# Where the transform's way back stands: beside attention's small scores, with attention's transposes in an experts' bank

## The reference, cut to what matters

```
x = x + xattn(LN(x), ctx)     # top-32 cross attention -> film -> FFT convolution -> film -> FFN
x = x + attn(LN(x))           # self attention over 32 tokens, one head, width 256
x = x + ffn(LN(x))            # 8 experts, top-2 gates, all experts computed
```

## Time and profile before

| | us |
|---|---|
| median of 3 runs | 606.03 |
| lowest and highest | 601.78, 606.12 |
| profiled execution | 601.4 |
| its span, first to last instruction | 599.6 |
| PE busy in the span | 551.3 |
| DVE busy | 498.0 |
| ACT busy | 293.2 |
| POOL busy | 280.6 |
| mean granted TensorE clock | 0.979 |

### The profile page before, as it was taken

How to read it: one execution, slowest core, us unless ns; L and a number is a source line. 1 busy time by engine, 2 the same in 40 slices (tenths; PEclk the granted TensorE clock), 3 DMA queues, 4 the chain that set the end, 5 groups by cost and what they waited for, 6 DMA issues and landing times.

```text
span 599.6 us, 13084 instructions
## 1 busy us (share of the span) xinstructions
PE 551.3 (92%) x4558; PEld 399.3 (67%) x4558; DVE 498.0 (83%) x1761; ACT 293.2 (49%) x768; POOL 280.6 (47%) x656
## 2 busy tenths in 40 slices
PE   3688488999999999999999999999999999989966
PEld 2344264768686777768686768686877768675845
DVE  7997876789898988989888989898988989876443
ACT  3032242464646564555646364646564555635432
POOL 6755147625445362626363535445362636262521
PEclk9998897999999999999999999999999999999998
DMA  8488103030403030210303030304030210000000
GB/s 282 65 325 338 66 2 119 2 113 2 131 2 131 1 110 22 74 60 23 109 19 113 19 113 10 123 1 131 3 129 3 83 50 10 2 10 1 10 1 17
DMA packets 17957, 42.33 MB, mean 71 GB/s; under 512 B 2770, under 2 KB 9570, under 8 KB 17380
## 3 DMA queue, kind: packets, MB, share of 16 engines
q1 hardware_dynamic: 17892, 41.51, 20.8%
HBM read 39.37 MB, written 2.13 MB: 69 GB/s over the span
## 4 chain that ended last, share of the span: by engine, by line
PE 78%; DVE 3%; issue 3%; ACT 2%; POOL 2%; POOLq 0%; DVEq 0%
PE BB L1128 10%; PE D L1128 9%; PE BB L1151 9%; PE D L1145 8%; PE SS L1108 4%; PE SS L1114 3%; PE PC L1269 2%; PE PC L1308 2%; PE BB L1229 2%; PE PC L1271 2%; PE BB L1230 2%; PE BB L1264 2%; PE BB L1263 2%; PE PC L1211 2%; PE BB L1246 2%
## 5 line engine op out<-in xcount | busy, mean ns | idle before, releaser
L545 POOL TENSOR_SCALAR var_in<-mv 128x1 f32<-128x1 f32 x64 | 14.0, 219 | 240.8 <-DVE mv L774 141.1
L809 DVE MATCH_REPLACE8 work<-top,work 128x257 f32<-128x257 f32 x192 | 77.4, 411 | 0.0
L1128 PE MATMUL D<-ang,e_w 128*128 128x128 f32 x512 | 71.2, 285 | 0.0
L803 DVE MAX8 top<-work 128x8 f32<-128x257 f32 x192 | 71.0, 411 | 0.0
L1128 PEld LDWEIGHTS D<-ang,e_w 128*128 128x128 f32 x512 | 63.2, 196 | 10.1 <-issue 10.1
L1128 PE MATMUL BB<-ang,w 128*128 128x128 f32 x512 | 66.4, 284 | 1.3 <-ACT ang L701 0.9
L1145 PE MATMUL D<-expw,ang 128*128 128x256 f32 x256 | 66.0, 388 | 1.2 <-ACT ang L620 0.9
L1128 PEld LDWEIGHTS BB<-ang,w 128*128 128x128 f32 x512 | 60.8, 195 | 8.4 <-ACT ang L701 7.4
L620 ACT ACTIVATE ang<-BB,cols 128x128 f32<-128x128 f32 x128 | 36.5, 367 | 46.8 <-PE BB L1128 46.8
L641 ACT ACTIVATE expo<-SS,nmax,srs 128x257 f32<-128x257 f32 x64 | 32.7, 561 | 52.7 <-DVE work L789 52.6
L1151 PE MATMUL BB<-expw,ang 128*128 128x256 f32 x256 | 57.9, 379 | 0.0
(11 more groups left out here) (258 smaller groups left out, 1230.7 us busy)
## 6 DMA issues: line engine op xcount, KB each, us to landing
ctx_n<-in_ctx_n SPq DMA_DIRECT2D x16, 768.0 KB, 4.3
ctx_t<-in_ctxT SPq DMA_DIRECT2D x16, 514.0 KB
ctx_t<-in_ctxT SPq DMA_DIRECT2D x16, 257.0 KB
xT<-in_xT SPq DMA_DIRECT2D x16, 128.0 KB, 2.5
x_all<-in_x SPq DMA_DIRECT2D x4, 512.0 KB, 8.6
out<-out_sb SPq DMA_DIRECT2D x16, 128.0 KB, 1.7
ctx_l<-in_ctx_l SPq DMA_DIRECT2D x16, 96.0 KB, 5.0
w<-in_W SPq DMA_DIRECT2D x1, 1024.0 KB
```

The source lines that it names most:

```text
L803: V.max(top[:, 2 * q + k, 8 * r8:8 * r8 + 8], work[:, 2 * q + k, :]).then_inc(chains["top"], 1)
L809: V.match_replace(work[:, 2 * q + k, :], top[:, 2 * q + k, 8 * r8:8 * r8 + 8], work[:, 2 * q + k, :], TAKEN).then_inc(chains["taken"], 1)
L1128: ins = MM(bank[:, 128 * m:128 * m + 128], w[:, k, at:at + 128], xs[:, 128 * k:128 * k + 128], start=k == 0, stop=k == 1)
```

## The change

It moves work in three engines' lists and changes one bank. The matmuls and the vector operations stay the same in number and shape; one activation of one column is added.

- TensorE: behind the end of the cross scores, the transposes of `xl2` come first and go to D0, an experts' bank, and wait until the experts' gelus have read that bank (g2b_a). Experts 0, 1 follow, then the qk_w and wv_w products (which now also wait for had_v), film's second half, the transform's way back, the small scores, and only then experts 2, 3.
- ScalarE: the copy of `xT2` reads D0 and stands ahead of the exps of the second pair of cross scores; a one-column Exp (`ahead`) comes before it when there is a tile a. The copy of `yb` stands behind those of `xmT` and `v_c`.
- VectorE: find8 and the row maximum of the small scores, which stood behind film and transform (L932 to L938), stand ahead of them.

```diff
 # ScalarE
-                if a:
-                    exps(a, 1)
                 if c:
+                    if a:
+                        A(ahead[:, :], b1[:, 0:1], ACT.Exp)
                     wait(act, s["xT2_mm"], one(c))
-                    copy(xT2[:, :], C0[:, 0:D], "xT2_a")
-                if b:
-                    wait(act, s["inv_mm"], one(b))
-                    copy(yb[:, :], B0[:, D:2 * D], "y_a")
+                    copy(xT2[:, :], D0[:, 0:D], "xT2_a")
+                if a:
+                    exps(a, 1)
                 if c:
                     wait(act, s["v_mm"], one(c))
                     A(xmT[:, :], C0[:, D:2 * D], ACT.Copy)
                     copy(v_c[:, :], C0[:, 0:D], "v_a")
+                if b:
+                    wait(act, s["inv_mm"], one(b))
+                    copy(yb[:, :], B0[:, D:2 * D], "y_a")
+                if c:
                     wait(act, s["nmaxc_v"], one(c))
 # VectorE
                 if a:
                     take8(a, 0, 2)
+                    find8(a, 0, 3)
+                if c:
+                    wait(dve, s["s_mm"], one(c))
+                    V.reduce_max(nmax_c[:, :], C0[:, D:D + T], AXX, negate=True).then_inc(s["nmaxc_v"], 1)
                 if b:
...
                     V.bn_aggr(mv[0][:, :], bn[0][:, :]).then_inc(s["st0_v"], 1)
-                if a:
-                    find8(a, 0, 3)
-                if c:
-                    wait(dve, s["s_mm"], one(c))
-                    V.reduce_max(nmax_c[:, :], C0[:, D:D + T], AXX, negate=True).then_inc(s["nmaxc_v"], 1)
                 if dd:
                     gated(range(2, 4))
 # TensorE
                 if a:
                     scores_end(a, 1)
+                if c:
+                    wait(pe, s["xl2_v"], one(c))
+                    if dd:
+                        wait(pe, s["g2b_a"], one(dd))
+                    elif a and a.n == 2:
+                        pe.wait_ge(s["route_a"], 1)
+                    transposes(D0, xl2, "xT2_mm")
                 if dd:
                     experts(range(0, 2))
-                if b:
-                    wait(pe, s["had_v"], one(b))
-                    for k in range(BT):
-                        ins = MM(B0[T * k:T * k + T, D:2 * D], dft_y[:, :], had[0:NF, k, :], ...)
-                    ins.then_inc(s["inv_mm"], 1)
-                if c:
-                    wait(pe, s["xl2_v"], one(c))
+                if c:
+                    wait(pe, s["xT2_a"], one(c))
                     wait(pe, s["x2_v"], c.count(1, 0))
-                    transposes(C0, xl2, "xT2_mm")
-                if b:
-                    MM(B1[:, :], zT1[:, :], film1[:, 512:1024], ...)
-                    MM(B1[:, :], zT2[:, :], film2[:, 512:1024], ...).then_inc(s["y_mm"], 1)
-                if c:
-                    wait(pe, s["xT2_a"], one(c))
+                    if b:
+                        wait(pe, s["had_v"], one(b))
                     ...                                  # products with qk_w and wv_w, then v_mm
-                if dd:
-                    experts(range(2, 4))
+                if b:
+                    wait(pe, s["had_v"], one(b))
+                    MM(B1[:, :], zT1[:, :], film1[:, 512:1024], ...)
+                    MM(B1[:, :], zT2[:, :], film2[:, 512:1024], ...).then_inc(s["y_mm"], 1)
+                if b:
+                    for k in range(BT):
+                        ins = MM(B0[T * k:T * k + T, D:2 * D], dft_y[:, :], had[0:NF, k, :], ...)
+                    ins.then_inc(s["inv_mm"], 1)
                 if c:
                     wait(pe, s["v_a"], one(c))
                     ...                                  # small scores, then s_mm
+                if dd:
+                    experts(range(2, 4))
                 if following:                            # query of the next tile
```

More of the change, by code:

```diff
@@ L676, in step @@
                     gelus(act2, 1, D0, e_b1, "e1b_mm", "g2b_a", dd)
+                if c:
+                    if a:
+                        A(ahead[:, :], b1[:, 0:1], ACT.Exp)
+                    wait(act, s["xT2_mm"], one(c))
+                    copy(xT2[:, :], D0[:, 0:D], "xT2_a")
                 if a:
@@ L679, in step @@
                 if c:
-                    wait(act, s["xT2_mm"], one(c))
-                    copy(xT2[:, :], C0[:, 0:D], "xT2_a")
+                    wait(act, s["v_mm"], one(c))
+                    A(xmT[:, :], C0[:, D:2 * D], ACT.Copy)
+                    copy(v_c[:, :], C0[:, 0:D], "v_a")
                 if b:
@@ L685, in step @@
                 if c:
-                    wait(act, s["v_mm"], one(c))
-                    A(xmT[:, :], C0[:, D:2 * D], ACT.Copy)
-                    copy(v_c[:, :], C0[:, 0:D], "v_a")
                     wait(act, s["nmaxc_v"], one(c))
@@ L1249, in step @@
                     scores_end(a, 1)
+                if c:
[5 more added lines that the diff above has]
+                    transposes(D0, xl2, "xT2_mm")
                 if dd:
                     experts(range(0, 2))
-                if b:
-                    wait(pe, s["had_v"], one(b))
-                    for k in range(BT):
-                        ins = MM(B0[T * k:T * k + T, D:2 * D], dft_y[:, :], had[0:NF, k, :], start=True, stop=True)
-                    ins.then_inc(s["inv_mm"], 1)
-                if c:
-                    wait(pe, s["xl2_v"], one(c))
-                    wait(pe, s["x2_v"], c.count(1, 0))
-                    transposes(C0, xl2, "xT2_mm")
-                if b:
-                    MM(B1[:, :], zT1[:, :], film1[:, 512:1024], start=True, stop=False)
-                    MM(B1[:, :], zT2[:, :], film2[:, 512:1024], start=False, stop=True).then_inc(s["y_mm"], 1)
                 if c:
                     wait(pe, s["xT2_a"], one(c))
+                    wait(pe, s["x2_v"], c.count(1, 0))
+                    if b:
+                        wait(pe, s["had_v"], one(b))
                     for m in range(2):
@@ L1272, in step @@
                     ins.then_inc(s["v_mm"], 1)
-                if dd:
-                    experts(range(2, 4))
+                if b:
+                    wait(pe, s["had_v"], one(b))
+                    MM(B1[:, :], zT1[:, :], film1[:, 512:1024], start=True, stop=False)
+                    MM(B1[:, :], zT2[:, :], film2[:, 512:1024], start=False, stop=True).then_inc(s["y_mm"], 1)
+                if b:
+                    for k in range(BT):
+                        ins = MM(B0[T * k:T * k + T, D:2 * D], dft_y[:, :], had[0:NF, k, :], start=True, stop=True)
+                    ins.then_inc(s["inv_mm"], 1)
                 if c:
```

## The result

The changed kernel takes 621.18 us, median of 4 runs (618.09 to 622.23), against 605.14 (601.78 to 606.12, 4 runs): ratio 1.027, 95% interval 1.023 to 1.031. It is slower by 16 us. The profiled execution took 622.23, its span 620.4. The first profile of before was a quick one (601.4), so a second one was taken later: 606.03, span 604.2. The changed kernel was profiled a second time as well: 620.60, span 618.8. Where the two kernels are compared in sum, these second profiles are used.

A forecast was written before the change was run, and what follows sets the result against it. TensorE, without a hole in full stages 3 to 15, was taken as the bound. 10.9 us over those 13 stages plus 3.1 elsewhere made 14.0 on 601.4, 615.4; with 2.3 for spread, 617.5 us, range 608 to 624.

The forecast's parts named there:

- The chain on VectorE: Row maximum, film, transform, gated adds and softmax behind the small scores hold TensorE before experts 6, 7: +0.84 us per full stage.
- rival 1: At experts 6, 7: TensorE stays full and the kernel is not slower, 598.4 or 600.7 us; chance 8%.
- TensorE's shapes: Way back and scores adjacent save two array shape changes per stage, about 0.1 us each; scores end at 326.86.
- The wait for xT2: Before the qk product, with only experts 0, 1 covering ScalarE's copy: just in time, taken as 0, ends 0 and 0.35 us.
- The other stages: Stages 1, 2, 16 and 17, outside the 13 full ones: together +3.1 us.
- Stage 1: Way back behind film's second half, find8 ahead of VectorE's block: +0.4 us.
- Stage 16: No new tile but the same VectorE chain from scores to expert 8; TensorE waited there already: +0.5 us.
- Stage 2: No experts; transposes of hn come later, behind VectorE's film and transform, root and hn: +1.5 us (0.8 to 1.8).
- Stage 17 and the rest: No film block; adds 2, 3 wait for experts 2, 3, now behind the scores: +0.65 us (0 to 0.96).
- Rival 3's clock: Stage 2's hole could halve TensorE's clock, losing 3.4 us once; with late xT2, 619 to 625 in all; chance 14%.
- the one for the spread between executions: Added to the total: 2.3 us, half the 4.6 between the profiled execution and the median 606.03.

## Why the prediction was right

**The chain on VectorE, +0.84 us a full stage: right**, measured 0.80 to 0.81, and 10.5 in 13 stages for 10.9. Read on the old stage's clock (subtract 8.06), the steps were: scores' end 326.86, measured 326.71; row maximum 327.02, measured 326.86; film's end 329.06, measured 329.03; TensorE on at 329.98, measured 329.94; hn's transposes 332.23, measured 332.19. Taking work away from that chain removes the hole, and moving work within it moves the hole. One part of the reasoning doesn't hold: the prediction laid the idle 1.1 us to VectorE's order, and let rival 1 win if film could run ahead of the row maximum. With that order put back film starts no sooner and the stage is 0.73 longer. What costs is TensorE's order: the way back starts at 334.04 - 8.06 = 325.98 where it started at 322.33. Besides, the weight load's idle time was taken too small, 1.20 us in place of about 0.9, where TensorE's own hole is 0.79.

**TensorE's shapes:** the scores came 0.15 sooner than taken because the way back needed 0.45 in front of the scores in place of 0.57. VectorE did not profit: film starts 0.13 later behind the row maximum than its old neighbours suggested (335.16 against 334.92 + 0.11). The prediction took film's operands to be there by then; the copy of the way back ended at 335.12, so film waits for it, as the run with VectorE's order put back shows in the open. Two errors of 0.15 and 0.13 cancelled, and that the term came out within 0.04 is in part luck.

**The wait for xT2: right at 0.** ScalarE's rows in the changed kernel show how near it was: the copy ends at 330.18, the qk product starts at 330.47 with no idle.

```profile
328.34 1.28 ACT L679 ACT_TABLE_LOAD   x1
...
329.80 0.38 ACT L615 ACTIVATE ang<-D 128x256 f32<-128x256 f32 x1
```

**The other stages, 3.1 us, partly wrong.** Stage 1 grew by 0.40 (from the first film product to hn's transposes 15.05 in place of 14.65), as forecast. Stage 16 grew by 0.5 (33.64 against 33.12), as forecast.

Stage 2 was to lose 1.5; the two second profiles give 32.55 against 32.05, +0.5. The step that failed is what hn waited for before. In the profile that the prediction read, GpSimd was free when film ended. In the second one it was still busy with a power of 24 columns (4.20 us, to 103.92) and what follows it, so hn's transposes waited 1.05 us there without the change.

Stage 17 and the rest were to lose 0.65 and lost 1.8. The wait of stage 17 itself was well taken, 0.84 within 0 to 0.96. The last stage's 1.0 stood in the sum at nothing, and so did the clock behind stage 17's wait, 1.67 where it falls.

**Rival 3's clock** did fall in stage 2, but in the kernel before too. In the changed kernel TensorE stood idle 2.65 us before the values' product and 1.05 before hn's transposes; then the clock was 0.65. In the second profile of before it stood idle 1.15 and 1.05, and then the clock was 0.64. The changed kernel's window stands first, that of before, again, second:

```profile
108.10:112.80 4.70, 4.64 (x26) 4.17 (x26) 2.90 (x14) 0.81 (x2) 0.87 (x3) 0.65 0.00 0
...
107.80:112.50 4.70, 4.68 (x26) 4.19 (x26) 3.56 (x15) 0.81 (x2) 1.46 (x4) 0.64 0.01 2
```

From hn's transposes to the next tile's query that is 4.6 to 4.7 us, in place of 3.4 in the first profile of before, where the clock was 1.00. So it costs 1.2 us, not 3.4, and between the second profiles nothing.

In stage 16 of the first profile of the changed kernel the granted clock was 0.62 in the stretch that holds a wait of 1.71 us for GpSimd:

```profile
548.91 1.09 PE L1195 MATMUL PC<-prob,wsel 128*32 128x257 f32 x8 [1.71 <-POOL wsel L572]
...
547.00:556.00 9.00, 7.29 (x49) 5.54 (x49) 2.98 (x10) 2.24 (x4) 3.41 (x9) 0.62 0.05 16
```

This wait is not the change's either. Before has it too (1.64 and 1.71 us), with 1.00 and 0.81 in the same piece of the stage (533.20 to 542.20 and 536.20 to 545.20), and the changed kernel's second profile has 0.81. So 35.05 against 33.64 is a matter of the execution. In the full stages a hole of 0.79 us left the clock at 1.00.

**The total:** 617.5 forecast, 621.2 measured; 615.4 was the sum on an execution that turned out to be the quickest kind. On the second profile's 606.0 the same sum gives 620.0. The term that was too small is the one for the spread between executions, 2.3 taken and 4.6 needed; it was half of the difference between two groups of executions, a guess. The change itself was taken as 14.0 and measured 16.0 between the medians, 14.6 between the second profiles.

## What to carry to other kernels

Before two pieces of work are put side by side on a full engine, ask what the second engine did while it waited for the later of them. Here 1.93 us of VectorE's work, with its operands, moved behind the very wait which that work used to fill, for a saving of 0.10 us of TensorE's time a stage. When a hole has a named releaser, move that item ahead once: if the hole reappears at the next wait, the bound is the sum of the chain, not an item of it. And before a difference between two profiles is put down to the change, or taken from it, look at the same piece of work in all profiles at hand.

## What the runs showed of the hardware

- A change of array shape on TensorE costs about 0.1 us in float32: four passes of 256 columns take 0.87 us between full-size neighbours, 0.96 before a 32-column group and 1.06 between a one-row and a 32-column one. With both groups 32 columns wide (96 rows, then 128) the first took 0.45 in place of 0.57, and the weight load of the second was already under way at 334.28, before its first matmul at 334.49.
- A wait of 1.62 us on TensorE in stage 17 was followed by a granted clock of 0.72 in six profiles and of 1.00 in three. One of 0.79 us in each full stage never was: there the clock stayed at 1.00.
- The same programs differ by up to 3.5 us in their first 83 us from run to run, with a granted clock of 1.00 shown over products that take nearly twice as long. The cause is open.
